# Four layers on one core: input in four pieces, fronts unrolled, the first stack ahead of the routing, gates behind the next maximum

## The reference

```python
xn = layernorm(x)                      # no gain, eps 1e-5
x = x + attention_l(xn) + feed_forward_l(xn)
```

## Time and profile before

| | |
|---|---|
| median of 3 runs | 2037.21 us (2028.65 to 2046.6) |
| the profiled execution | 2040.47 us, span 2038.3 us |
| layer 0 / 1 / 2 / 3 begin at (first transpose) | 29.8 / 708.4 / 1062.5 / 1589.8 us |
| busy: TensorE, VectorE, ScalarE, GpSimd | 79%, 60%, 38%, 19% of the span |
| mean granted TensorE clock | 0.882 |

### The profile page before, as it was taken

How to read it: one execution, slowest core, us unless ns; L and a number is a source line. 1 busy time by engine, 2 the same in 40 slices (tenths; PEclk the granted TensorE clock), 3 DMA queues, 4 the chain that set the end, 5 groups by cost and what they waited for, 6 DMA issues and landing times.

```text
span 2038.3 us, 43880 instructions
## 1 busy us (share of the span) xinstructions
PE 1606.7 (79%) x12679; PEld 1014.2 (50%) x12679; DVE 1229.8 (60%) x3480; ACT 779.5 (38%) x1739; POOL 386.3 (19%) x488
## 2 busy tenths in 40 slices
PE   3286799999775759999984588888875598888888
PEld 2122476666422358888873145555531245555554
DVE  6454465655655656666775456666644566666664
ACT  2022355444332423333331155555533144444444
POOL 2274210100445201111132400000034100000000
PEclk9866799999877759999995599999987599999999
DMA  8021466566222000000000133333320011111110
GB/s 237 26 77 45 126 185 204 167 203 180 65 56 54 3 0 1 0 0 0 0 1 30 60 120 115 114 115 113 115 79 20 27 44 43 41 41 41 41 41 14
DMA packets 133432, 145.06 MB, mean 71 GB/s; under 512 B 15144, under 2 KB 114272, under 8 KB 133088
## 3 DMA queue, kind: packets, MB, share of 16 engines
q1 hardware_dynamic: 101088, 106.20, 17.2%
q10 hardware_dynamic: 26112, 25.17, 4.2%
q0 software_dynamic: 6144, 12.60, 2.1%
HBM read 104.65 MB, written 39.52 MB: 71 GB/s over the span
## 4 chain that ended last, share of the span: by engine, by line
PE 52%; DVE 22%; issue 13%; another core or an unknown queue 4%; ACT 2%; DMA 2%; POOL 2%; DVEq 1%; SPq 1%; ACTq 0%; POOLq 0%
PE pO L704 7%; PE pT_ L572 6%; PE pH L598 6%; PE pY L606 5%; PE pH L504 5%; DVE X L1314 4%; DVE mx L1281 3%; PE pS L651 3%; PE pS L673 3%; DVE stk L1287 2%; PE pT_ L494 2%; PE pT_ L570 2%; PE pT_ L561 1%; PE pS L537 1%
## 5 line engine op out<-in xcount | busy, mean ns | idle before, releaser
L814 ACT ACTIVATE pex<-pT_ 128x512 f32<-128x512 f32 (+1 forms) x768 | 427.8, 562 | 650.6 <-PE pT_ L572 316.3
L1281 DVE TENSOR_REDUCE mx<-pS 128x2 f32<-128x512 f32 x512 | 346.9, 689 | 205.4 <-PE pS L549 98.7
L572 PE MATMUL pT_<-stk 32*128 32x256 f16 x1024 | 204.5, 290 | 88.1 <-DVE mx L1281 47.0
L549 PE MATMUL pS<-stk 32*128 32x256 f16 x1024 | 214.6, 298 | 31.5 <-DMA stk<-packed_qk 19.5
L704 PE MATMUL pO<-pex,va 128*9 128x256 f32 (+1 forms) x3072 | 205.9, 389 | 2.0 <-ACT pex L814 2.0
L911 POOL TENSOR_TENSOR qk<-qkf,qk 128x512 f16<-128x512 f32 x48 | 55.6, 1158 | 724.8 <-DVE qk L1257 364.0
L807 ACT ACTIVATE wb<-pH,b 128x256 f32<-128x256 f32 x256 | 107.5, 471 | 198.5 <-PE pH L504 198.5
L572 PEld LDWEIGHTS pT_<-stk 32*128 32x128 f16 x1024 | 55.4, 94 | 216.1 <-DVE mx L1281 94.1
L819 ACT ACTIVATE xts<-pO 128x256 f32<-128x256 f32 x192 | 74.0, 385 | 181.5 <-PE pO L704 123.5
L504 PE MATMUL pH<-XT,w 128*128 (+1 forms) x512 | 136.4, 390 | 0.0
L598 PE MATMUL pH<-xsT,wb 128*128 128x128 f32 x888 | 129.9, 290 | 1.8 <-ACT hbs L785 1.8
(11 more groups left out here) (195 smaller groups left out, 2828.6 us busy)
## 6 DMA issues: line engine op xcount, KB each, us to landing
wb<-in_w SPq DMA_DIRECT2D x111, 514.0 KB, 3.8
stk<-packed_qk ACTq DMA_DIRECT2D x96, 256.0 KB, 2.7
packed_qk<-qk SPq DMA_DIRECT2D x144, 128.0 KB, 2.0
xsb<-sorted_x SPq DMA_DIRECT2D x111, 64.0 KB, 3.4
sorted_y<-ysb SPq DMA_DIRECT2D x111, 64.0 KB, 3.0
sorted_x<-wb SPq DMA_DIRECT2D x3, 1536.0 KB, 13.3
w<-in_w SPq DMA_DIRECT2D x2, 1024.0 KB, 7.7
out<-X SPq DMA_DIRECT2D x16, 128.0 KB, 1.8
```

The costliest lines, as they stand in the source:

```text
L549: return pe.matmul(bank[:, part * T:(part + 1) * T], stk[rows, side, j, part * P:(part + 1) * P], stk[rows, side, j, T:2 * T], start=True, ...
L572: return pe.matmul(bank[:, part * T:(part + 1) * T], key, stk[rows, side, j, 0:T], start=True, stop=True)
L814: act.activation(pex[:, k % 8, 0:n], bank[:, 0:n], ACT.Exp).then_inc(s("T_free"), 1)
L1281: ins = dve.tensor_reduce(mx[:, :, j, col], bank.rearrange("p (c n) -> p c n", c=2), AX.X, ALU.max)
```

## The change

- X is loaded in four pieces with a semaphore each. SP raises only the 18 shared semaphores ahead of them and the other 67 behind. VectorE waits for each piece as it comes to it.
- The fronts are unrolled. VectorE normalizes once, into `XN`, in all layers. ScalarE copies once, to `XT`, and TensorE takes the router's operand from there. TensorE turns group g and then makes the logits of group g-1.
- The choice is made for tiles 0 to 15 (`choose(l, 0)`) and 16 to 31 apart; ScalarE makes the first half's exponential behind group 6's logits and the second's at the end.
- In layers 0 and 2 turn -2 stands between `choose(l, 0)` and the rest of the routing, on TensorE and VectorE (`behind_first`), and GpSimd and ScalarE begin it at once; GpSimd waits for the slots at the end of turn -2, ahead of its scatters. The gates are passed ahead of `start_search`.
- In layers 2 and 3 VectorE writes q and k once, and GpSimd makes the f16 halves (line 909's cast), as in layer 0.
- In layer 3 VectorE's two products of step H come behind its next maxima (`gate`), or ahead of Y, E, or D where the turn has no S.

```diff
-def run_turns(eng, layer, body, unlooped=0):
+def run_turns(eng, layer, body, unlooped=0, behind_first=None):
 
     last = B if layer == 1 else B + 1
     loop_from, loop_to = LOOPS[layer][0], LOOPS[layer][1] - unlooped
     for n in range(-2, loop_from):
         body(Turn(layer, n))
+        if n == -2 and behind_first is not None:
+            behind_first()
     with eng.Fori(0, (loop_to - loop_from) // 2) as loop:
         for par in range(2):
             body(Turn(layer, loop_from + par, loop))
...
-            "ld_x": [(X[:, 0:16, :], xin[:, 0:16, :]), (X[:, 16:32, :], xin[:, 16:32, :])],
+            **{f"ld_x{c}": [(X[:, 8 * c:8 * c + 8, :], xin[:, 8 * c:8 * c + 8, :])] for c in range(4)},
...
-                with pe.Fori(0, NT // 4 // 2) as turn:
...
+                def turned(g):
+                    pe.wait_ge(sem("xn_ready"), PRIMED + l * (NT // 4) + g + 1)
+                    pe.wait_ge(sem("xts_ready"), PRIMED + l * (NT // 4) + g - 1)
+                    for u in range(4):
+                        ins = pe.transpose(pS[:, g % 2, u * P:(u + 1) * P], XN[:, 4 * g + u, :], ident[:, :])
+                    ins.then_inc(sem("turned"), 1)
+                def logits(g):
+                    pe.wait_ge(sem("xts_ready"), PRIMED + l * (NT // 4) + g + 1)
+                    pe.wait_ge(sem("logits_copied"), PRIMED + min(l, 3) * (NT // 4) + g - 1)
+                    for u in range(4):
+                        t = 4 * g + u
+                        ins = pe.matmul(pT_[:, g % 2, u * 16:u * 16 + EXPERTS[l]], XT[:, t * P:(t + 1) * P],
+                                        wr[l][:, :], start=True, stop=True)
+                    ins.then_inc(sem("logits"), 1)
+                for g in range(NT // 4 + 1):
+                    if g < NT // 4:
+                        turned(g)
+                    if l < 3 and g > 0:
+                        logits(g - 1)
...
+                if l == 1:
+                    pe.wait_ge(sem("gates"), PRIMED + l + 1)
+                def rank_tokens():
                     pe.wait_ge(sem("chosen"), 1 + SORTED.index(l))
+                    pe.wait_ge(sem(f"L{l}_S_free"), PRIMED + ring_uses(l, "S", -2))
                     every = rb[:, :, :].rearrange("p t e -> p (t e)")[:, 0:8 * NT]
                     pe.matmul(pS[:, 0, 0:8 * NT], tri[:, :], every, start=True, stop=True)
                     pe.matmul(pS[:, 1, 0:8 * NT], onesm[:, :], every, start=True, stop=True)\
                       .then_inc(sem("ranked"), 1)
-                if l == 3:
-                    pe.wait_ge(sem("w3_ready"), 3)
-                pe.wait_ge(sem("xts_ready"), PRIMED + (l + 1) * (NT // 4))
-                if l < 3:
                     pe.wait_ge(sem("gates"), PRIMED + l + 1)
-                run_turns(pe, l, take_turn)
+                run_turns(pe, l, take_turn, behind_first=rank_tokens if l in SORTED else None)
...
+            def exponents(l, part):
+                half = slice(NT // 2 * part, NT // 2 * (part + 1))
+                act.wait_ge(sem("shifted"), PRIMED + 2 * l + part + 1)
+                act.activation(pr[:, half, 0:EXPERTS[l]], ra[:, half, 0:EXPERTS[l]], ACT.Exp)\
+                   .then_inc(sem("exp_logits"), 1)
             def phase_a(l):
-                s = lambda n: sem(f"L{l}_{n}")
...
+                for g in range(NT // 4 + 1):
+                    if g < NT // 4:
+                        act.wait_ge(sem("turned"), PRIMED + l * (NT // 4) + g + 1)
+                        act.activation(XT[:, g * 4 * P:(g + 1) * 4 * P], pS[:, g % 2, :], ACT.Copy)\
                            .then_inc(sem("xts_ready"), 1)
-                    if l < 3:
...
+                    if l < 3 and g > 0:
+                        act.wait_ge(sem("logits"), PRIMED + l * (NT // 4) + g)
+                        act.activation(LG[:, (g - 1) * 4:g * 4, 0:EXPERTS[l]],
+                                       pT_[:, (g - 1) % 2, 0:64].rearrange("p (u e) -> p u e", e=16)[:, :, 0:EXPERTS[l]],
+                                       ACT.Copy).then_inc(sem("logits_copied"), 1)
+                    if l < 3 and g >= NT // 4 - 1:
+                        exponents(l, g - NT // 4 + 1)
...
                 pool.wait_ge(sem("xts_ready"), PRIMED + (l + 1) * (NT // 4))
-                if l < 3:
+                if l == 1:
...
-                                halves = [0, 1]
-                            else:
-                                halves = [1]
+                            halves = [0, 1]
...
-                    if turn.n == -2:
+                    if turn.n == -2 and l in SORTED:
+                        if l == 0:
+                            pool.wait_ge(sem("places_zeroed"), 16 * -(-MAXBLOCKS // ZEROED_BLOCKS))
+                        pool.wait_ge(sem("places_ready"), 1 + SORTED.index(l))
                         scatter(sorts)
...
-                with dve.Fori(0, NT // 4 // 2) as turn:
...
+                for g in range(NT // 4):
+                    dve.wait_ge(sem("rstd"), PRIMED + l * (NT // 4) + g + 1)
+                    for t in range(4 * g, 4 * g + 4):
+                        ins = dve.tensor_scalar(XN[:, t, :], X[:, t, :], MV[:, t, 0:1], rstd[:, t:t + 1],
+                                                ALU.subtract, ALU.mult)
+                    ins.then_inc(sem("xn_ready"), 1)
+            def choose(l, part):
                 n = EXPERTS[l]
-                full_e = lambda a: a[:, :, None].to_broadcast([P, NT, n])
-                lg, p_, a_, b_, c_, g_, k_ = (x[:, :, 0:n] for x in (LG, pr, ra, rb, rc, GA, rank))
-                dve.wait_ge(sem(f"ld_{l}"), full[f"ld_{l}"])
-                dve.wait_ge(sem("logits_copied"), PRIMED + l * (NT // 4) + NT // 4)
+                half = slice(NT // 2 * part, NT // 2 * (part + 1))
+                full_e = lambda a: a[:, half, None].to_broadcast([P, NT // 2, n])
+                lg, p_, a_, b_, c_, g_, k_ = (x[:, half, 0:n] for x in (LG, pr, ra, rb, rc, GA, rank))
+                m1, m2 = r1[:, half], r2[:, half]
...
+            def routing(l):
+                choose(l, 1)
                 if l == 1:
 
                     chain.link(dve.memset(GA[:, :, 15:16], 1.0))
-                if l == 0:
-                    start_search()
                 if l in SORTED:
                     places(l)
                 dve.sem_inc(sem("gates"), 1)
+                if l == 0:
+                    start_search()
...
+                    if t < NT and not gathered and t % 8 == 0:
+                        dve.wait_ge(sem(f"ld_x{t // 8}"), 16)
...
+                ungated, scores = [], any(kind == "S" for kind, _, _ in turn.steps)
+                def gate():
+                    for k, local in ungated:
+                        dve.wait_ge(s("tanh_done"), PRIMED + use_h + local + 1)
+                        dve.wait_ge(s("Y_full"), PRIMED + use_y)
+                        tc.link(dve.scalar_tensor_tensor(hg[:, k % 2, :], th[:, k % 2, :], 1.0, pH[:, k % 2, 0:T],
+                                                         ALU.add, ALU.mult))
+                        dve.scalar_tensor_tensor(hb[:, k, 0:T], hg[:, k % 2, :], 0.5, pH[:, k % 2, T:2 * T],
+                                                 ALU.mult, ALU.mult).then_inc(s("H_free"), 1)
+                    ungated.clear()
                 for kind, k, local in turn.steps:
+                    if kind in "YE" or (kind == "D" and not scores):
+                        gate()
...
-                            for to in (qkf[:, 0, side], qk16[:, 1 + k, :]):
...
+                            if l == 2:
+                                ins = dve.tensor_scalar(qkf[:, 0, side], bank[:, 0:T],
+                                                        rope2[:, k, bass.ds(turn.row(2), 1)], None, ALU.mult)
+                            else:
+                                ins = dve.tensor_scalar(qkf[:, 0, side], bank[:, 0:T], bq3[:, k:k + 1],
+                                                        QSCALE if k == 0 else 1.0, ALU.add, ALU.mult)
                         ins.then_inc(s("S_free"), 1)
...
                         ins.then_inc(s("S_free"), 1)
+                        gate()
...
+                        ungated.append((k, local))
...
                 if l < 3:
+                    dve.wait_ge(sem(f"ld_{l}"), full[f"ld_{l}"])
+                    choose(l, 0)
+                if l == 1:
                     routing(l)
                 if l == 1:
...
-                run_turns(dve, l, lambda turn: take_turn(turn, tc))
+                run_turns(dve, l, lambda turn: take_turn(turn, tc),
+                          behind_first=(lambda: routing(l)) if l in SORTED else None)
...
+            of_x = [group for group in loads if group.startswith("ld_x")]
+            shared = [name for name in primed if name in SHARED_SIGNALS]
+            for name in shared:
+                sp.sem_inc(sem(name), PRIMED)
+            load_inputs(of_x)
             for name in primed:
```

(7 more changed lines are left out.)

102 lines of the change are left out of this document (19 added, 83 removed).

## The result

The changed kernel takes 1970.57 us (median of 4 runs, 1968.01 to 1971.12) against 2035.88 of the kernel before on the same chip (4 runs, 2028.65 to 2046.6): a ratio of 0.967, 95% interval 0.964 to 0.971. It is faster by 65 us. The forecast said 1988, a gain of 49, with a range from 1972: the direction was right, the size too small.

What follows compares the result with a forecast made beforehand. No engine bounds the whole; the fronts and layer 3's turns, where TensorE waits for VectorE, can be won. Terms 20.5 - 1.2 + 4.2 + 4.7 + 21.1 = 49.3 off 2040.5, less 3.3, give 1988 us; range 1972 to 2010.

Steps and rivals of the forecast that it cites:

- layer 3's front: Normalizing to first projection: with XN as target VectorE runs through, 11.6 us instead of 16.6; gain 4.7 (3 to 6).
- layer 1's front: First transpose to first matmul behind the gates: halving costs more than it hides, 45.0 against 43.8 us, -1.2 (-4 to +1).
- Input in pieces: Start of layer 0: four pieces issued earlier let statistics begin at 10.1 us; gain 7.3, loop heads some 0.5.
- TensorE's work of a front closes up to its busy sum, 21.95 us: Fronts, unrolled and crossed: TensorE's work takes 21.95 us, half one's exponential comes 21.1 us behind the first transpose.
- The clock: TensorE in the fronts stays at clock 0.50 (1.2 GHz); a rise there was a rival at 1958 us, 5%.
- Turns of layer 3: Layer 3's turns of 25.14 us lose 1.45 each in 14 turns and 0.8 in turn 14: 21.1 us (8 to 30).
- J1's wait isn't worth its size: Layer 3's turns: of J1's 1.01 us wait for J0's evacuation behind the gates, only VectorE's 0.24 at P0 goes.
- 0.4 for the f16 copy ahead of P1: Layer 3's turns: taking VectorE's f16 copy from ahead of P1 gains 0.4 us a turn.
- The gates' 1.06: Layer 3's turns: moving the gates gains 0.24 us at P0 and 0.82 at V1 a turn.
- Rival 1: Layer 3's turns: gates' move worth nothing, VectorE is full and hands its backlog on; 0.8 a turn left, 1998 us; 18%.
- Rival 4: Layers 2 and 3: the cast makes the stack late, ScalarE waits 3.84 us in 28 turns, 108 lost, 2046 us; 3%.
- turns of layers 0 to 2: nothing: Stretches behind the fronts of layers 0 to 2 counted as 0 gain; layer 2's turns 0 (0 to 5).

Runs made afterwards that it cites:

- the table of the four corners: Layer 3's turn with gates at H, copies by VectorE 25.29 us, by GpSimd 24.99; with gates behind the next maximum 23.81 and 23.83, by GpSimd 23.72.
- The run that was to tell the packets from GpSimd's issuing: The kernel before with layer 2's scatters moving only the first 16 of 128 rows of each tile; 1940.17 us against 1938.78.

## Why the forecast was right in kind and too small

The gain was 65 us for 49. In the two traces the miss is 22.8: 5.5 in the fronts of layers 0 to 2, 2.1 in layer 3's front, 4.2 behind it, 11.0 in the three stretches that the sum left at nothing. Against the medians 6.8 of that is the chance of the two executions (72.1 against 65.3). Two terms had the wrong sign, layer 1's front (1.0 gained for 1.2 lost) and the 0.7 for the cast in layer 2. The others were too small, and much of that is one kind of reading: a length or a busy time was taken from rows whose neighbours overlap, or where waits stand between them, and one turn was taken for the mean.

**Input in pieces:** right, 7.80 us for 7.3 + 0.5. The table load that was to delay the start by 1.0 did not: it runs at 0.71 us, long before ScalarE is needed.

**Fronts of layers 0 to 2: the step that failed is "TensorE's work of a front closes up to its busy sum, 21.95 us".** Closed up, the same work is busy for 20.07, because the last matmul of a run no longer counts with its whole length ahead of a wait. The exponentials came 2.4 us (layer 2) to 3.6 (layer 0) earlier than worked out. In layer 1 that is the whole miss (42.76 for 45.0). In layer 0 3.0 of the 3.6 were lost again. 1.8 of them stand in the routing's second half, where two steps of VectorE that read two tiles of SBUF last 1.35 and 1.03 us instead of 0.29, each beside GpSimd's sum and subtraction of the first stack:

```profile
49.49 1.26 POOL L902 TENSOR_TENSOR qkf<-qkf 128x512 f32<-128x512 f32 x1 [27.07 <-DVE qkf L1254]
49.56 1.35 DVE L1001 TENSOR_TENSOR ra<-LG,r 128x128 f32<-128x128 f32 x1
51.62 1.15 POOL L912 TENSOR_TENSOR qk<-qkf,qk 128x512 f16<-128x512 f32 x1
51.89 1.03 DVE L1005 TENSOR_TENSOR pr<-pr,r 128x128 f32<-128x128 f32 x1
```

They repeat to 0.01 us in four more traces with the stack ahead of the routing (among them the second of the changed kernel) and are not there in the run that takes the stack behind it. So the new order has a cost that the forecast did not see. Another 0.8 stands between the last slot (70.57) and the first scatter (71.61), for which it had 0.2; the placing itself took its 11.7. In layer 2 2.1 are left (38.82 for 40.9). That the halves cost more than they hide was right, in layer 1 (2.3 us by the run with the routing whole), and holds in layer 0 as well (2.2), and so does the reason, ScalarE's order: moved, the exponential gives 5.8 in layer 1.

**The clock** was right where it counted: 0.50 (1.2 GHz) through the 20 us of layer 1's front with TensorE busy throughout, and in layer 2's too. The Trainium skill, "TensorE: Matmul & The Clock Gate", section "What's actually happening", has activity release the throttle; these 20 us disagree. For layer 0's front the windows print another level:

```profile
22.00:42.10 20.10, 20.10 (x97) 19.73 (x98) 8.63 (x35) 6.35 (x16) 0.42 (x1) 1.00 0.98 304
```

Its matmuls do not bear that 1.00 out: four transposes last 1.09 us (at 25.50) as in layer 1's front at 0.50, while at a granted 1.00 in layer 3 they last 0.66. By these lengths layer 0's front ran at the lower level, as the forecast took it; a granted clock is best checked against the length of a known matmul.

**Layer 3's front: 6.8 for 4.7.** From the first normalizing (1548.58) to the first projection (1558.32) it takes 9.7 us, not 11.6. 1.4 of the difference is VectorE's: the forecast made 9.7 us out of 0.30 a tile, the mean of a row of six that overlap (1.81 / 6), and the 32 tiles take 8.30, one starting 0.26 behind the other. The clock gives 0.45: it rose behind 4 us in which TensorE transposed without a gap, and the last group's transposes, the ones that count, last 0.66 us (at 1556.93) for 1.11. In answer to the earlier trace rows, VectorE and the first projection in the timeline, and two windows of the changed kernel:

```profile
1548.58 8.30 DVE L986 TENSOR_SCALAR XN<-X,MV,rstd 128x128 f32<-128x128 f32 x32 [0.17 <-DVE MV L1185]
...
1558.32 1.10 PE L656 MATMUL pS<-XT,wq 128*128 128x256 f32 x4 [0.73 <-issue]
```

```profile
1553.00:1557.00 4.00, 3.15 (x17) 2.13 (x18) 3.88 (x16) 2.74 (x5) 0.00 (x0) 0.82 0.02 4
1557.00:1560.00 3.00, 1.97 (x9) 1.12 (x9) 0.92 (x2) 0.79 (x2) 0.00 (x0) 1.00 0.00 0
```

On the third chip the same front took 11.09 us at 0.50, paced by GpSimd's reciprocals (1.33 a group), and gave 4.4. That this is nearly the forecast's 4.7 is luck: the reciprocals' pace, which the forecast did not have, takes back what VectorE's shorter steps give. There GpSimd's weights of layer 3 end at 1460.3 us, 1.3 ahead of the first normalizing, and the reciprocals queue behind them; on the first chip they end 20 us ahead (1528.1 and 1548.6).

**Turns of layer 3: the split of 1.45 us was wrong, the turn itself right.** The forecast had turns of 23.7 us, and they last 23.72. The old turn was longer than its base of 25.14: the turns alternate between 25.16 and 25.45, 25.29 in the mean, so a turn gave 1.57. That is 1.7 of the 4.2 us missing here; another 2.0 came ahead of turn 0 (1.19 up to turn -1's stack write, 0.77 in turn -1), for which the sum had nothing. All together gave 25.3 (24 on average over the runs) for 21.1. "J1's wait isn't worth its size" holds in part: it fell by 0.77 (1.01 to 0.24), and that is followed by a new wait of 0.47 at the scores behind P0. "0.4 for the f16 copy ahead of P1" failed: by the table of the four corners the copies give 0.3 beside the old gates and 0.1 beside the moved ones, and P1's wait goes with the gates alone. The gates' 1.06 is 1.3 to 1.5. Rival 1, the gates' move worth nothing, was the opposite of what the runs show. Rival 4 was also added up wrong: 1988 and 108 lost is 2096, not 2046; it did not come.

**The cast on GpSimd** held up next to nothing. By the Trainium skill's "SBUF — State Buffer", section "Who interferes with whom", work of GpSimd that reads SBUF and a step of VectorE with two inputs from SBUF shut each other out, so it could have cost an estimated 0.6 us each. The 48 casts of the changed kernel last 609 to 699 ns. Of the 32 in layers 2 and 3, 31 run beside VectorE's maxima and copies, which keep their lengths, and one holds a two-input step of the routing by 0.16 us (0.45 for 0.29); the turns of layer 3 with them are 0.1 shorter than without. The trace agrees with that rule, only at other work than the forecast looked at: the two steps of layer 0 above, and in the trace of before already a step of VectorE at 592.39 that lasts 0.62 us for 0.35 beside a cast. ScalarE never waited for the packing in layers 2 and 3.

**What the sum left at nothing** gave 4.1, 4.0 and 2.9 us in the first pair of traces. The step "turns of layers 0 to 2: nothing" was right in layer 0 as far as can be told, and wrong by 1.3 and about 4 in the other two.

- Layer 0's 4.1 is within what it varies by (611.6 to 617.4 on one chip for kernels with the same layer 0).
- Of layer 1's 4.0, 1.3 is the change's own. In all four traces of the old order the third turn lasts 18.74 us (one more dip apart), every second one after it 18.95, and 5.82 pass before layer 2's first transpose; in the ten with the new fronts it is 18.42, 18.82 and 5.48, but for that with the routing whole (18.92) and dips. What shortens them no run tells apart. The rest is dips of the clock, 1.7 us each, three in the first trace of before and one in the first of the changed kernel. Over all traces this stretch takes 306.5 to 310.3 us in the old order and 303.4 to 307.8 in the ten others.
- Layer 2's belongs to the order of the stack, on two of the three chips: 481.5, 482.3, 484.9 and 485.5 us with the scatters ahead of turn -2's projections, 477.2 to 479.7 with them behind and distributed as in the changed kernel; on the third, 443.4 and 443.7. It goes with the late starts, which the forecast did not see although the trace of before had them.

The sum of what is the change's own, with the means of the runs: 7.8 + 13.3 + 1.0 + 1.3 + 6.9 + 4.4 to 6.8 + 24 = 59 to 61 us; with 4.4 it is the third chip's 58.5. On the first chip the higher end and layer 2's late starts, 3.6 by its traces, make 65. The medians vary by a few us, so that this comes out to the us is in part luck.

**Open:** what releases VectorE and ScalarE late on two chips. The kernel before counts 69.2 us of VectorE's and 55.7 us of ScalarE's idle time under a releaser that the profile doesn't know (groups of waits: us, times, longest), the changed kernel 62.3 and 51.9 us in the same two groups. Most of it lies in layer 0's first turns and in the tails of layers 0 and 2:

```profile
DVE mx L1281 <- remote: 69.2, 13, 24.0
ACT xts L819 <- remote: 55.7, 9, 26.1
```

None of the four traces of the third chip has such a wait. The run that was to tell the packets from GpSimd's issuing fell on that chip and cannot.

## What to carry to other kernels

When an engine is full and another waits for it at several places of a loop, list the waits of a whole period and look at which of them one backlog feeds: moving the work that makes the backlog shrank or took away three waits, none of which the profile had put down to that work. Halving a step so that one half hides costs its fixed share at once (0.29 us for half the columns of a 0.42 us step) and pays only if the half really begins early; look at what stands ahead of it in every engine's order. The busy time of matmuls with waits between them is no floor for a closed-up stretch, and a mean length out of a row of overlapping steps is too long: count from start to start. When work of GpSimd moves beside other work of VectorE, look at what VectorE reads there; two steps here took 1.8 us more for it. And take the base of a turn from its mean over a whole period, not from one turn.
